# Sending the tokens of six batches through memory to their two experts, instead of multiplying them by all eight

## The reference

```python
# per token x (256 channels), E = 8 experts, TOP_K = 2
logits = x @ Wr.T + br                    # 8 router logits
p      = softmax(logits)                  # the two largest are kept and scaled to a sum of 1
y      = sum over the two chosen e of  gate[e] * (We[e] @ x + be[e])
out    = y @ Wo.T + bo                    # then added to the residual stream
```

## Time and profile before

| | |
|---|---|
| median of 3 runs | 654.12 us (652.51 to 654.73) |
| profiled execution, its own time | 654.19 us |
| its span in the profile | 652.4 us |
| PE busy | 570.7 us, 87% of the span |
| DVE busy | 475.4 us, 73% |
| ACT / POOL busy | 46% / 18% |
| chain that ended last | PE 50%, DVE 24% |

### The profile page before, as it was taken

The page is one execution under the profiler, slowest core; times in us unless marked ns, Lnnn a source line. Parts: engine busy times, 40 slices in busy tenths (PEclk is TensorE's granted clock), DMA queues, the critical chain, the costliest instruction groups (busy, mean ns, idle before and its releaser), DMA issues.

```text
span 652.4 us, 10840 instructions
## 1 busy us (share of the span) xinstructions
PE 570.7 (87%) x3994; PEld 385.1 (59%) x4032; DVE 475.4 (73%) x1273; ACT 300.3 (46%) x472; POOL 118.6 (18%) x115
## 2 busy tenths in 40 slices
PE   9884776867989989989889888999999999999897
PEld 4743433745766756757667666656575756565443
DVE  4677868857678687787876776786968778786664
ACT  2346677626555455554545554243343425253110
POOL 2121000351313313313223132103030200000000
PEclk9886899889999999999999998999999999999999
DMA  9600000574135043143143240405032140000000
GB/s 335 258 1 1 1 0 2 127 220 128 52 98 150 28 123 114 56 132 113 35 146 89 59 146 19 127 1 162 2 100 62 41 122 16 2 17 1 17 18 16
DMA packets 40636, 51.15 MB, mean 78 GB/s; under 512 B 4180, under 2 KB 33620, under 8 KB 40276
## 3 DMA queue, kind: packets, MB, share of 16 engines
q1 hardware_dynamic: 40584, 50.46, 25.8%
HBM read 35.63 MB, written 14.68 MB: 77 GB/s over the span
## 4 chain that ended last, share of the span: by engine, by line
PE 50%; DVE 24%; issue 3%; DMA 1%; SPq 1%; ACT 1%; POOL 1%; DVEq 0%; ACTq 0%
PE ps L1317 13%; PE ps L1204 8%; PE ps L1196 7%; DVE nmax L1466 7%; PE ps L1279 4%; PE ps L1267 3%; PE ps L1247 3%; DVE xn L1422 2%; PE ps L1263 2%; PE ps L1188 2%; DVE stats L1411 2%; DVE acc L1551 2%; PE ps L1286 2%; PE ps L1242 2%; PE ps L1239 1%
## 5 line engine op out<-in xcount | busy, mean ns | idle before, releaser
L1466 DVE TENSOR_REDUCE nmax<-ps 128x2 f32<-128x512 f32 (+1 forms) x192 | 130.5, 681 | 70.5 <-PE ps L1247 67.7
L1368 ACT ACTIVATE PT<-ps 128x512 f32<-128x512 f32 x192 | 114.0, 597 | 145.3 <-PE ps L1267 143.2
L1317 PE MATMUL ps<-wm,xnT 128*128 128x512 f32 x256 | 120.1, 600 | 0.0
L1362 ACT ACTIVATE QS<-ps 8x1024 bf16<-8x1024 f32 x64 | 65.0, 1016 | 31.3 <-PE ps L1252 30.1
L1267 PE MATMUL ps<-QS,KS 110*128 110x256 bf16 (+3 forms) x512 | 75.0, 248 | 0.0
L1551 DVE SCALAR_TENSOR_TENSOR acc<-ps,gate,acc 128x256 f32<-128x256 f32 x128 | 61.6, 481 | 16.5 <-PE ps L1317 14.2
L1317 PEld LDWEIGHTS ps<-wm,xnT 128*128 128x128 f32 x256 | 44.6, 190 | 38.3 <-issue 38.0
L1263 PE MATMUL ps<-fixb 128*128 128x256 bf16 (+1 forms) x192 | 60.2, 314 | 7.5 <-DVE nmax L1466 3.5
L1148 POOL TENSOR_TENSOR rstd<-ve,fix 128x2 f32<-128x2 f32 x31 | 21.5, 693 | 247.9 <-DVE ve L1417 247.9
L1196 PE MATMUL ps<-xnT,by_dim 128*128 128x256 f32 x256 | 62.6, 390 | 2.2 <-ACT xnT L1333 2.2
L1168 POOL TENSOR_TENSOR parts<-rest,fix 128x512 bf16<-128x512 f32 x30 | 38.0, 1268 | 139.1 <-DVE rest L1435 100.5
(11 more groups left out here) (217 smaller groups left out, 882.8 us busy)
## 6 DMA issues: line engine op xcount, KB each, us to landing
parts_dram<-parts SPq DMA_DIRECT2D x32, 384.0 KB, 3.1
QS<-parts_dram SPq DMA_DIRECT2D x96, 128.0 KB
KS<-parts_dram SPq DMA_DIRECT2D x96, 128.0 KB, 2.6
wt<-wt_dram SPq DMA_DIRECT2D x1, 2562.0 KB, 19.2
wm<-wm_dram SPq DMA_DIRECT2D x1, 2449.0 KB, 13.0
xc<-x_dram SPq DMA_DIRECT2D x8, 256.0 KB, 5.3
out_dram<-res SPq DMA_DIRECT2D x8, 256.0 KB, 2.1
w<-w_dram SPq DMA_DIRECT2D x1, 845.0 KB, 7.5
```

The source lines that it names most:

```text
L1317: mm = pe.matmul(d, normT(stage, batch)[:, c, t * P:(t + 1) * P], M("We", c * EXPERTS * CH + e * 2 * CH, 2 * CH), start=(c == 0), stop=(c ...
L1362: act.activation(QS[MAX_AT:MAX_AT + MAX_ROWS, stack(stage, batch), 4 * n:4 * n + 4, :], bank(piece)[MAX_AT:MAX_AT + MAX_ROWS, 0:PIX].unsqu ...
L1368: act.activation(PT[:, pt_slot(piece, n), :], bank(piece), ACT.Exp).then_inc(drain(piece), 1)
L1466: dve.tensor_reduce(group[:, 0, :] if part == 0 else group[:, 1, 2 * part - 2:2 * part], bank(piece).rearrange("p (j n) -> p j n", n=w_), ...
```

## The change

Batches 6 and 7 keep the eight E pieces. Batches 0 to 5 (`SENT`) lose them. Instead:

- RK, SL, SC: after the gates of a batch, PE counts with three small matmuls how many earlier tokens chose each expert, DVE makes from that a row number for each of the token's two copies, and POOL sends the 256 tokens of `xn`, twice, to these rows of a memory area `by_expert`: four indirect DMAs of 128 rows. Each expert has a region of its own. LNb of the next batch waits for them (`rows_sent`), as it overwrites `xn`.
- BL: behind batch 5, DVE works out for 32 blocks of 128 rows which expert and which rows each has.
- BD, BT, BY, BS, in 16 pairs of blocks, one pair a step from step 38 of body 5 on: SP reads a block's row from a register (a register load) and loads it; PE turns it (four transposes a pair), ACT copies it out; PE reads the block's expert into a register and multiplies the block by that expert's weights alone (two matmuls of 256 columns a block); ACT copies the result out, SP stores it over the block in memory.
- GA, CB, CT: when all blocks are stored, POOL fetches for each batch 0 to 5 its rows, four indirect DMAs of 128 rows a batch; DVE adds them to the sum, each times its gate; then CT as before.
- E of batches 6 and 7 move to steps 44 to 51 (`DENSE_AT`), the fetches of batches 0 to 5 stand between those of batch 6.
- In the first part SP fills `by_expert` (13312 rows of 1 KB) with zeros from a zeroed tile, and DVE waits for that before it writes the tile.

```diff
+WAVES = ((0, 1, 2, 3, 4, 5),)
+FIRST_PAIR = (38,)
+PAIRS_IN, PAIRS_TURNED, PAIRS_OUT = 3, 2, 2
+DENSE_AT = {6: range(44, 52), 7: range(44, 52)}
...
+    out += [("RK", 3, 0, 31), ("SL", 3, 0, 32), ("SC", 3, 0, 32)]
+    end = start + apart * pairs(wave) + 2
+    if batch == last:
+        out.append(("BL", 3, 0, 32))
+        for k in range(pairs(wave)):
+            at = start + apart * k
+            out += [("BD", 3, k, at - 3), ("BT", 3, k, at), ("BY", 3, k, at + 1), ("BS", 3, k, at + 1)]
+    at = end + BODY * (last - batch) + (batch - WAVES[wave][0])
+    out += [("GA", 3, 0, at), ("CB", 3, 0, at + 1), ("CT", 3, 0, at + 2)]
...
+                sp.wait_ge(padded_zero, 2)
+                sp.wait_ge(wt_loaded, 16)
+                    sp.dma_start(rows.rearrange("(p a r) n -> p a (r n)", p=P, r=4),
+                                 zeros.unsqueeze(1).broadcast_to([P, all_rows(w) // P // 4, 4 * CH])).then_inc(rows_zeroed, 16)
...
+                    if k == 2:
+                        dve.wait_ge(rows_zeroed, 16 * len(WAVES))
...
+                if kind == "BD":
+                    wait(sp, "blocks_ready", ("BL", stage, batch, 0))
+                    wait(sp, "rows_sent", ("SC", stage, batch, 0))
+                    if pair_before(piece, PAIRS_IN):
+                        full(sp, ("BT", *pair_before(piece, PAIRS_IN)))
+                    for j in range(2):
+                        k = 2 * n + j
+                        row_value[w, k] = sp.value_load(block_row[0:1, w, k:k + 1], min_val=0, max_val=all_rows(w) - P)
+                        sp.dma_start(rows_in[:, pair_at(piece, PAIRS_IN), j], by_expert[w][bass.ds(row_value[w, k], P), :])\
...
+                if kind == "SC":
+                    wait(pool, "slots_ready", ("SL", stage, batch, 0))
+                    for k in range(2):
+                        for t in range(2):
+                            pool.indirect_dma_start(by_expert[wave_of(batch)][:, :],
+                                                    bass.IndirectOffsetOnAxis(slots[:, batch, k, t:t + 1], 0),
+                                                    xn[:, 1, t, :], None).then_inc(sems["rows_sent"], 16)
+                if kind == "GA":
...
+                        wait(pool, f"block_stored{pair_at(sent, PAIRS_OUT)}", sent)
+                    wait(pool, "combined", before(("CB", stage, batch, 0), 2))
...
+                            pool.indirect_dma_start(fetched[:, par, t, k, :], None, by_expert[w][:, :],
+                                                    bass.IndirectOffsetOnAxis(slots[:, batch, k, t:t + 1], 0))\
...
+                if kind == "BY":
+                    drained(pe, ("BT", stage, batch, n))
...
+                    for j in range(2):
+                        at = pe.value_load(block_expert[0:1, w, k:k + 1], min_val=0, max_val=(EXPERTS - 1) * CH)
+                        for c in range(NC2):
+                            weights = M("We", c * EXPERTS * CH, EXPERTS * CH)
+                            mm = pe.matmul(d[:, j * CH:(j + 1) * CH], turned_in[:, pair_at(piece, PAIRS_TURNED), j, c, :],
+                                           weights[:, bass.ds(at, CH)], start=(c == 0), stop=(c == 1))
...
+                if kind == "CB":
+                    wait(dve, f"rows_fetched{par}", ("GA", stage, batch, 0))
+                    for k in range(2):
+                        for t in range(2):
+                            op = dve.scalar_tensor_tensor(into, fetched[:, par, t, k, :], gains[:, batch, k, t:t + 1], into,
```

More of the change, by code:

```diff
@@ L8 @@
 I32 = mybir.dt.int32
+U32 = mybir.dt.uint32
 ALU = mybir.AluOpType
@@ L77, with wave_of, room, all_rows @@
 TURN_BACK = (7, 6)
+WAVES = ((0, 1, 2, 3, 4, 5),)
+SENT = sum(len(w) for w in WAVES)
+FIRST_PAIR = (38,)
+PAIR_STEP = (1,)
+PAIRS_IN, PAIRS_TURNED, PAIRS_OUT = 3, 2, 2
+def wave_of(batch):
+    return next(k for k, w in enumerate(WAVES) if batch in w)
+def room(wave):
+    return len(WAVES[wave]) * PIX
+def all_rows(wave):
+    return EXPERTS * room(wave) + EXPERTS * P
+def pairs(wave):
+    blocks = (2 * room(wave) + EXPERTS * (P - 1)) // P
+    return (blocks + 1) // 2
 PARTS_OF_MAX = 2
@@ L161, in in_order, with last_of_wave, pair_number, pair_at @@
     return [piece for _, piece in sorted(out)]
-JOBS = ("S", "M", "X", "T", "Q", "K", "V", "PR", "FF", "R", "GT", "GB", "E", "CT")
-SETTLED = {"LNa": 2, "MS": 1, "AT": 1, "R": 1, "RT": 3, "E": 1}
+JOBS = ("S", "M", "X", "T", "Q", "K", "V", "PR", "FF", "R", "GT", "GB", "E", "CT", "RK", "BT", "BY")
+SETTLED = {"LNa": 2, "MS": 1, "AT": 1, "R": 1, "RT": 3, "E": 1, "SL": 2, "BL": 9, "CB": 1}
+def last_of_wave(batch):
+    return batch == WAVES[wave_of(batch)][-1]
+def pair_number(piece):
+    return sum(pairs(w) for w in range(wave_of(piece[2]))) + piece[3]
+def pair_at(piece, ring):
+    return pair_number(piece) % ring
+def pair_before(piece, by):
+    at = pair_number(piece) - by
+    for w, batches in enumerate(WAVES):
+        if 0 <= at < pairs(w):
+            return 3, batches[-1], at
+        at -= pairs(w)
+    return None
 def settled(piece):
-    return SETTLED.get(piece[0], 0) + (piece[0] == "RT" and piece[3] == 3)
+    kind, batch, n = piece[0], piece[2], piece[3]
+    if kind == "RT" and n == 3:
+        return 4 + (batch < SENT and not last_of_wave(batch))
+    return SETTLED.get(kind, 0)
 def signals(piece, bank):
@@ L1145, in pool_piece @@
                 kind, stage, batch, n = piece
+                par = batch % 2
                 if kind == "LNa":
@@ L1323, in tensor_piece @@
+                if kind == "CT":
+                    if batch < SENT:
+                        wait(pe, "combined", ("CB", stage, batch, 0))
+                    else:
+                        drained(pe, ("E", stage, batch, 7))
+                        drained(pe, ("E", stage, batch, 3))
+                    mm = turn4(X[:, 2 * batch:2 * batch + 2, :])
                 if kind in JOBS:
@@ L1420, in vector_piece @@
                     full(dve, ("T", stage, batch - 1, 0))
+                    if stage == 3 and 0 < batch <= SENT:
+                        wait(dve, "rows_sent", ("SC", stage, batch - 1, 0))
                     for t in range(2):
@@ new lines, in vector_piece @@
+                if kind == "CB":
+                    wait(dve, f"rows_fetched{par}", ("GA", stage, batch, 0))
+                    for k in range(2):
+                        for t in range(2):
+                            into = X[:, 2 * batch + t, :]
+                            op = dve.scalar_tensor_tensor(into, fetched[:, par, t, k, :], gains[:, batch, k, t:t + 1], into,
+                                                          ALU.mult, ALU.add)
+                        if k == 0:
+                            settle(op)
+                    op.then_inc(sems["combined"], 1)
```

186 lines of the change are left out of this document (170 added, 16 removed), and 3 rows, old and new, of the table FLOW.

## The result

Before: 653.32 us median (650.49 to 654.73, 4 runs). After: 701.90 us (698.78 to 703.47, 4 runs), ratio 1.074 with an interval of 1.069 to 1.080: 7.4% slower (forecast 689, range 641 to 728). The profiled execution has a span of 700.3 us against 652.4.

The account below looks back on a forecast made before the run. PE was taken as the bound, with waits that E covered coming out. PR of batch 6 at 552 (36 ahead), first pair 560, 16 pairs 74, tail 53.8: span end 688, plus 1.8 gives 689 us; range 641 to 728.

Parts of the forecast that it names:

- Bodies: Batches 0 to 4: 28.1 us without E, 1.6 for small DVE operations, 1 for sending tokens; 31 us a body.
- 28.1 for the body without experts: First stage-2 body of the old trace, 30.0 us, less 1.9 for its one E; taken for bodies preparing queries and keys.
- the sending 1: In each body, POOL's four indirect DMAs ahead of the SPLITs make the next layer norm and `xn` late: 1 us.
- The last two bodies: The two bodies before PR of batch 6, preparing no queries or keys: 23 us, and 25 with BL.
- To the first pair: From SL at 548: four indirect DMAs 4.4 us, landing 2.1, SP's two loads and their landing; first pair at 560.
- The pair: Transposes, ACT's copy, register load 1.1, weights, two blocks in a row: 4.6 us, SP just hidden at 4.2.
- The tail: After the last pair: stores, 24 indirect DMAs at 1.1 us, sums, CT, E of batch 7, end: 53.8 us.
- Zeros: Zero fill of 13.6 MB in the first part ends near 67 us, before DVE asks at 86.85: costs nothing.
- Rival 1: Bodies 28 and 21 us, pairs 3.7, indirect DMAs 0.51, all at lower prices: 642 us, 1.9% faster; chance 0.14.
- Rival 2: Whole kernel: PE's work alone decides, by spreading over the waits, saving 46 us: 608 us; chance 0.05.
- Rival 4: Whole kernel: gains and losses meet, nothing to measure, 652 to 656 us; chance 0.06.
- Rival 3: PE at half clock among pairs, judged by earlier clocks from 40 to 60 us: 37 us more, 726; shared chance 0.13.

## Why the prediction held, step by step

It had the sign and the mechanism: waits that E covered come out, and pairs and fetches stand in a row where E had filled PE. The time lies 13 us above the forecast and in its own range. That it is not further off is partly luck: to the first pair 14.5 us were missing in the sum and in the tail 6.4, and the pairs gave 8.6 back. The kernel was to be 36 us ahead at the PR of batch 6 and was 18 ahead (570.4 against 588.6). The steps in the profiled execution:

| | forecast | measured |
|---|---|---|
| PR of batch 4 | 504 | 516.1 |
| PR of batch 6 | 552 | 570.4 |
| first pair | 560 | 574.5 |
| 16 pairs | 74 | 65.4 |
| last pair's end to span's end | 54 | 60.4 |
| span's end | 688 | 700.3 |

- **Bodies, 31 forecast, 33.8 measured.** Of the terms, 28.1 for the body without experts was 30.8, the small operations 1.6 were nothing, and the sending 1 was 3.1. The first term failed at the 1.9 us taken off for the one E of the first body in the earlier trace rows. That E stood on PE from 409.89 to 411.83, beside DVE's last steps to the PR and not on the way to it (the rows below are of the kernel before), so taking it away shortens nothing: without any E the bodies took 30.5 to 31.3 us, at a clock of 0.89 to 0.94. The sending failed in the route, not only the size: I looked for a late layer norm, and that was on time (POOL idled for 1.9 us ahead of it); what came late was the SPLITs, and the split of the maxima with them.

```profile
409.65 0.69 DVE L1466 TENSOR_REDUCE nmax<-ps 128x2 f32<-128x512 f32 x1 [2.64 <-PE ps L1247]
411.43 0.68 DVE L1498 TENSOR_TENSOR xt<-ps,X 128x512 f32<-128x512 f32 x1
```

- **The last two bodies, 23 and 25 forecast, 24.9 and 29.3.** Their floor was nearly right (22.2 and 22.0 without experts). BL was sized as 2 us of DVE's time and took 3.2 (560.05 to 563.20); in the rows PE waits 4.66 us for `attnT` behind it and then does PR's 8 matmuls at half clock in 3.75 us, not 1.89: some 6.5. That BL makes this wait is read from the rows; no run leaves it out alone.

```profile
564.82 3.75 PE L1360 MATMUL ps<-wo,attnT 128*128 128x256 f32 x8 [4.66 <-DVE attnT L1701]
```

- **To the first pair, 8 us forecast, 4.1.** SL and the sending ran ahead of the late PR of batch 6, and SP's first register load began at 568.0.
- **The pair, 4.6 forecast, 4.1.** The parts stand in the rows as in the sum. The register load with its operations took 0.8, not 1.1, and the second hardly showed (products 2.01, not 2.13). The Trainium skill (DMA: Bandwidth & Descriptors, section "Latency and other measured facts") has a floor of 600 ns for it; by that the sum was to be 8 us less. The pairs were 8.6 less; the load itself took 0.33 at the median, below the page's figure, and the measurement decides. SP beside it was hidden, at 3.3 and not 4.2.
- **The tail, 54 forecast, 60.4.** The indirect DMA took 0.95 to 0.96 us on POOL, less than the 1.1, but 0.30 lies between two: 24 in 30.6 us and not 26.4. E of batch 7 began at half clock, 14.9 instead of 13.9, and from the last fetch to it 6.5 passed, not 4.7.
- **Zeros.** Hidden: 13312 KB landed in 35.5 us, and DVE waited 0.63 us at 85.5, for ACT.
- **Rivals.** Rival 1 needed all of its low prices, and none came: bodies 33.8 (28), pairs 4.1 (3.7), a fetch 1.26 with its pause (0.51). Rival 2, PE's work alone (608), is ruled out from below: even without the experts of six batches 618.65. Rival 4 is out by the 7.4%. Rival 3 was right in kind and wrong in place. The clock stayed at 1.00 among the pairs, though PE works for 19.0 of 30 us there (607 to 637), and fell in the bodies, where it works for 27.4 of 33.9. The longest wait among those pairs was 1.8 us, those ahead of the falls in the bodies 2.13 and 2.73. But the length of one wait does not settle it either: with E of batch 7 ahead of the turns, PE waits 2.87 us in the tail and the clock stays at 1.00. No run here says what decides; the comparison with 40 to 60 us did not foretell it.

## What to carry to other kernels

Work that leaves a full engine uncovers the waits that it hid, and TensorE then pays twice where its clock falls behind them: price the stage without the work by a run that leaves it out, not by a row that still holds some of it. Instructions put ahead of others in an in-order queue delay what follows them there, so look at which chain starts behind it; the sending cost 3.1 us a body in one place and 0.9 three steps later. Split work that needs a round trip (load, turn, copy, load a register, multiply) so that the next item's first half stands ahead of this one's second half, and leave enough dense work for the waits at the end.

## What the runs showed of the hardware

- DVE's small operations on 8 columns, 0.17 us elsewhere, took 0.88 and 1.18 beside POOL's SPLIT, and ended with POOL's operations to 0.03 us; without the sending they were 0.17 again. The Trainium skill (SBUF — State Buffer, section "Who interferes with whom") says that DVE and GpSimd (here POOL) share a pair of ports, as a lock for a whole instruction, so that the later one waits; the rows agree.
- A register load on PE (0.33 us, 0.8 with the operations behind it) is free when PE's queue has work ahead of it and costs 0.82 behind a wait.
- Eleven matmuls without a use, in a wait of 2.7 us, shortened a body by 2.5 us: behind that wait the clock no longer fell (0.95 to 1.00 over a body, 0.85 to 0.90 without them).
